# Attention on one core: score units merged to 18 steps a quad, score pairs in blocks of three

## The reference

```
x_proj = layernorm(x) @ Wqkv + bqkv                 # 16 heads of 16
att = where(causal, q @ k.T / sqrt(16), -inf)       # q, k, v = x_proj split and RESHAPED to (B, 16, T, 16)
y = softmax(att) @ v
x = x + y @ Wproj + bproj
```

## Time and profile before

| | us |
|---|---|
| median of 3 runs (lowest, highest) | 3928.14 (3921.84, 3932.45) |
| profiled execution, span | 3930.1 |
| attention, from the first pair to the last, about | 1077 to 3303 |

### The profile page before, as it was taken

One profiled execution on the slowest core, in us unless ns is written; L12 is line 12 of the kernel. 1 busy time (PEld: TensorE's weight loads), 2 busy tenths in 40 slices (PEclk: granted clock), 3 DMA queues, 4 the chain that ended last, 5 costly groups with the idle time before them and its releaser, 6 DMA issues. The chain is left out here.

```text
span 3930.1 us, 77952 instructions
## 1 busy us (share of the span) xinstructions
PE 3667.3 (93%) x26062; PEld 2353.8 (60%) x26062; DVE 2960.1 (75%) x9275; ACT 2237.0 (57%) x4407; POOL 1663.9 (42%) x2027
## 2 busy tenths in 40 slices
PE   6998999998689999999999999999999997999997
PEld 5887766665445555555555555555555554666664
DVE  8998577675677788788778878878877884576675
ACT  1100565555166666666666666666666665556654
POOL 2332132333445555554555545556455520132323
PEclk9999999999699999999999999999999998999999
DMA  2333122111877776877768777687876752121211
GB/s 71 102 101 103 43 65 65 46 57 35 158 112 114 112 117 107 121 109 115 123 108 116 117 112 118 105 126 104 117 122 110 101 71 61 34 69 60 65 39 49
DMA packets 701469, 361.31 MB, mean 92 GB/s; under 512 B 305072, under 2 KB 668080, under 8 KB 701104
## 3 DMA queue, kind: packets, MB, share of 16 engines
q1 hardware_dynamic: 701104, 356.65, 50.8%
HBM read 204.49 MB, written 150.99 MB: 90 GB/s over the span
## 5 line engine op out<-in xcount | busy, mean ns | idle before, releaser
L1839 ACT ACTIVATE att_probs<-att_s 128x512 f32<-128x512 f32 (+1 forms) x2560 | 1319.3, 557 | 755.3 <-PE att_s L1928 430.9
L1719 DVE CUSTOM_DVE_ANT_0 att_s<-att_s,att_above 128x384 f32<-128x384 f32 (+3 forms) x2048 | 958.0, 514 | 189.0 <-PE att_s L1958 188.9
L1980 PE MATMUL att_s<-att_qs,att_ks 49*128 49x512 f32 (+3 forms) x3072 | 917.9, 388 | 90.0 <-ACT att_probs L1839 29.1
L1958 PE MATMUL att_s<-att_ks,att_qs 48*128 48x512 f32 (+3 forms) x3072 | 964.2, 407 | 5.8 <-DVE att_maxima L1722 3.7
L1980 PEld LDWEIGHTS att_s<-att_qs,att_ks 49*128 49x128 f32 x3072 | 459.7, 185 | 650.9 <-ACT att_probs L1839 433.6
L1722 DVE TENSOR_REDUCE att_maxima<-att_s 128x1 f32<-128x512 f32 x1024 | 668.8, 682 | 225.6 <-PE att_s L1958 219.3
L2008 PE MATMUL att_o_ps<-att_probs,att_vs 128*32 128x512 f32 (+3 forms) x6144 | 632.1, 499 | 0.5 <-ACT att_probs L1839 0.5
L1958 PEld LDWEIGHTS att_s<-att_ks,att_qs 48*128 48x128 f32 x3072 | 487.6, 188 | 25.1 <-DVE att_maxima L1719 8.0
L1097 PE MATMUL ffn_h2p<-ffn_h,ffn_w 128*128 128x512 f32 x768 | 363.3, 595 | 3.0 <-ACT ffn_h L968 0.9
L1928 PE MATMUL att_s<-att_mask,att_places 64*128 64x64 bf16 (+1 forms) x3072 | 332.5, 205 | 0.0
L1719 DVE DVE_READ_ACCUMULATOR2_ANT att_maxima<- 128x1 f32 x2048 | 290.0, 142 | 0.0
(11 more groups left out here) (292 smaller groups left out, 6331.1 us busy)
## 6 DMA issues: line engine op xcount, KB each, us to landing
att_staged<-qk_scratch SPq DMA_DIRECT2D x768, 128.0 KB, 7.5
qk_scratch<-att_parts SPq DMA_DIRECT2D x128, 512.0 KB, 3.7
ffn_x<-x SPq DMA_DIRECT2D x64, 512.0 KB, 5.2
ssm_x<-in_L_attn_a_x_dram SPq DMA_DIRECT2D x32, 512.0 KB, 3.8
x<-ssm_y SPq DMA_DIRECT2D x32, 512.0 KB, 3.0
x<-ffn_y SPq DMA_DIRECT2D x32, 512.0 KB, 2.9
att_x<-x SPq DMA_DIRECT2D x32, 512.0 KB, 12.3
v_scratch<-att_v_tok SPq DMA_DIRECT2D x32, 512.0 KB, 3.4
```

Source lines behind the costliest of these rows:

```text
L1719: last = v.tensor_tensor_reduce(scores, scores, above[:, CH - w:CH], 1.0, -3.0e38, ALU.add, ALU.max, to)
L1839: a(probs[u % 2][2 * g + p][:, 0:n], bank[:, 0:n], ACT.Exp).then_inc(exp_done, 1)
L1958: last = mm(bank[:, col:col + w], rows_of(qs[buf], g, KROWS, p, BT * blk, BT * (blk + 1)), rows_of(ks[buf], g, KROWS, p, t0, t1), start=k ...
L1980: last = mm(bank[:, col:col + w], rows_of(ks[buf], g, SHIFT + 1, p, BT * j, BT * (j + 1)), rows_of(qs[buf], g, SHIFT + 1, p, t0, t1), star ...
```

## The change

- The two 256-wide units of `PASS2` become one of two pieces, so a quad has 9 units and 18 steps (36 halves), and each half of pass 2 has a partner of pass 1. The piece (6, 48, 64) belongs to the second half of the queries, so its product with V moves into `times_v` of unit 3 (`TIMES_V`).
- TensorE issues pairs in blocks of three. Only behind a block come an other work (in 8 of 12 blocks, `X_SLOTS`), then a `times_v` (9 a quad: `TIMES_V_SLOTS`, and the previous quad's last one behind block 0). Behind blocks 2, 3, 4, 8 and 10 come both.
- `probs` gets a third set, and an exponential waits for the `times_v` of three units back.
- VectorE and ScalarE order their tasks by halves instead of steps.

```diff
-    PASS2 = [[(0, 0, 32)], [(1, 8, 32), (3, 24, 32)], [(2, 16, 32)],
+    PASS2 = [[(0, 0, 32)], [(1, 8, 32), (3, 24, 32)], [(2, 16, 32), (6, 48, 64)],
              [(0, 32, 64)], [(1, 32, 64)], [(2, 32, 64)], [(3, 32, 64)], [(4, 32, 64)],
-             [(5, 40, 64), (7, 56, 64)], [(6, 48, 64)]]
-    FIRST_U2, LAST_U2 = (0, 3), (2, 9)
+             [(5, 40, 64), (7, 56, 64)]]
+    FIRST_U2, LAST_U2 = (0, 3), (2, 8)
+    TIMES_V = [[(u, n) for n in range(len(PASS2[u])) if (u, n) != (2, 1)] + ([(2, 1)] if u == 3 else [])
+               for u in range(len(PASS2))]
+    PROBS = 3
+    BLOCK = 3
+    X_SLOTS = (1, 2, 3, 4, 6, 8, 9, 10)
+    TIMES_V_SLOTS = {2: 0, 3: 1, 4: 2, 5: 3, 7: 4, 8: 5, 10: 6, 11: 7}
...
-        heads = [] if first and q == 0 else [(1, "heads", 0), (7 if q == 1 else 5, "heads", 1)]
-        finish = [] if first else {0: [(9, "turn", 0), (11, "out", 0), (13, "turn", 1), (15, "out", 1)],
-                                   1: [(3, "turn", 2), (5, "turn", 3), (9, "out", 2), (11, "out", 3)]}.get(q, [])
-        project = {0: [(3, 6), (7, 7)], 1: [(13, 0), (15, 1)], 2: [(3, 2), (7, 3), (9, 4), (11, 5), (13, 6), (15, 7)],
-                   3: [(3, 0), (7, 1), (9, 2), (11, 3), (13, 4), (15, 5)]}[q] if (more2 if q == 3 else more) else []
+        heads = [] if first and q == 0 else [(0, "heads", 0), (3 if q == 1 else 2, "heads", 1)]
+        finish = [] if first else {0: [(4, "turn", 0), (5, "out", 0), (6, "turn", 1), (7, "out", 1)],
+                                   1: [(1, "turn", 2), (2, "turn", 3), (4, "out", 2), (5, "out", 3)]}.get(q, [])
+        project = {0: [(1, 6), (3, 7)], 1: [(6, 0), (7, 1)], 2: [(1, 2), (3, 3), (4, 4), (5, 5), (6, 6), (7, 7)],
+                   3: [(1, 0), (3, 1), (4, 2), (5, 3), (6, 4), (7, 5)]}[q] if (more2 if q == 3 else more) else []
+        return [(BLOCK * X_SLOTS[n] / 2, kind, which)
+                for n, kind, which in sorted(heads + finish + [(n, "project", j) for n, j in project])]
...
-                            tasks += [(step, lambda unit=unit: maxima(4 * b + q + unit[0], unit[1]))]
+                            for g in (1, 0):
+                                tasks += [(step + (1 - g) / 2,
+                                           lambda unit=unit, g=g: maxima(4 * b + q + unit[0], unit[1], (g,)))]
...
-                    if g == 0 and (old or u >= 2):
-                        act.wait_ge(pv_done, UNITS2 * quad + u - 1)
+                    if g == 0 and (old or u >= PROBS):
+                        freed = u - PROBS + 1
+                        act.wait_ge(pv_done, UNITS2 * quad + (freed + 1 if u == 2 + PROBS else freed))
...
-                            tasks += [(step, lambda step=step, g=g: exponentiate(quad, q, step, g, not first or q > 0))]
+                            tasks += [(step + g / 2, lambda step=step, g=g: exponentiate(quad, q, step, g, not first or q > 0))]
...
-                    use = s2_use(q, step, g)
-                    if use >= 3 or not first:
-                        before = 3 if use >= 3 else (1, 4, 4)[use]
-                        pe.wait_ge(exp_done, 2 * STEPS * quad + 2 * step + g - before + 1)
+                    if s2_use(q, step, g) >= 3 or not first:
+                        pe.wait_ge(exp_done, 2 * STEPS * quad + 2 * step + g - 2)
...
+                            if (2 * step + g) % BLOCK != BLOCK - 1:
+                                continue
+                            part = (2 * step + g) // BLOCK
                             for n, (at, kind, which) in enumerate(events):
-                                if g == 0 and at == step - 1:
+                                if at == BLOCK * part / 2:
...
-                            if g == 0 and step % 2 and (step >= 3 or old):
-                                u = (step - 3) // 2
-                                if u >= 0:
-                                    times_v(quad, q, b, u, old)
-                                else:
-                                    times_v(quad - 1, (q - 1) % 4, b if q else b - 1, UNITS2 - 1, True)
+                            if part == 0 and old:
+                                times_v(quad - 1, (q - 1) % 4, b if q else b - 1, UNITS2 - 1, True)
+                            if part in TIMES_V_SLOTS:
+                                times_v(quad, q, b, TIMES_V_SLOTS[part], old)
```

More of the change, by code:

```diff
@@ L1236, in x_events @@
     def x_events(q, first, more, more2):
-        heads = [] if first and q == 0 else [(1, "heads", 0), (7 if q == 1 else 5, "heads", 1)]
-        finish = [] if first else {0: [(9, "turn", 0), (11, "out", 0), (13, "turn", 1), (15, "out", 1)],
-                                   1: [(3, "turn", 2), (5, "turn", 3), (9, "out", 2), (11, "out", 3)]}.get(q, [])
-        project = {0: [(3, 6), (7, 7)], 1: [(13, 0), (15, 1)], 2: [(3, 2), (7, 3), (9, 4), (11, 5), (13, 6), (15, 7)],
-                   3: [(3, 0), (7, 1), (9, 2), (11, 3), (13, 4), (15, 5)]}[q] if (more2 if q == 3 else more) else []
-        return sorted(heads + finish + [(s, "project", j) for s, j in project])
+        heads = [] if first and q == 0 else [(0, "heads", 0), (3 if q == 1 else 2, "heads", 1)]
[5 more added lines that the diff above has]
+                for n, kind, which in sorted(heads + finish + [(n, "project", j) for n, j in project])]
     def flags(b):
@@ L1283, in attention_phase @@
         full = [sb(f"full{k}", [P, CH]) for k in range(FULLS)]
-        probs = [[sb(f"probs{k}_{i}", [P, CH]) for i in range(4)] for k in range(2)]
+        probs = [[sb(f"probs{k}_{i}", [P, CH]) for i in range(4)] for k in range(PROBS)]
         o_sb = sb("o", [P, 2, CH])
@@ L1707, in low, with maxima @@
                         v.memset(carrier[:, :], 0.0).then_inc(freed, 1)
-                def maxima(quad, unit):
+                def maxima(quad, unit, groups=(1, 0)):
                     p, pieces, n = unit // len(PASS1), PASS1[unit % len(PASS1)], 2 * (UNITS1 * quad + unit)
-                    for g in (1, 0):
+                    for g in groups:
                         dve.wait_ge(s1_full, n + 2 - g)
@@ L1724, in maxima @@
                         last.then_inc(s1_free, 1)
-                    if unit % len(PASS1) == len(PASS1) - 1:
+                    if unit % len(PASS1) == len(PASS1) - 1 and groups[-1] == 0:
                         dve.wait_ge(s1_free, n + 2)
@@ L1834, in exponentiate @@
                     act.wait_ge(s2_full, 2 * STEPS * quad + 2 * step + g + 1)
-                    if g == 0 and (old or u >= 2):
-                        act.wait_ge(pv_done, UNITS2 * quad + u - 1)
+                    if g == 0 and (old or u >= PROBS):
+                        freed = u - PROBS + 1
+                        act.wait_ge(pv_done, UNITS2 * quad + (freed + 1 if u == 2 + PROBS else freed))
                     n = sum(HD * (t1 - t0) for _, t0, t1 in PASS2[u])
                     bank = s2_ps[s2_use(q, step, g) % 3]
-                    a(probs[u % 2][2 * g + p][:, 0:n], bank[:, 0:n], ACT.Exp).then_inc(exp_done, 1)
+                    a(probs[u % PROBS][2 * g + p][:, 0:n], bank[:, 0:n], ACT.Exp).then_inc(exp_done, 1)
                 def project(hb, j, index):
@@ L2001, in times_v @@
                         pe.wait_ge(v_loaded[s], 16 * (turn + 1))
-                    col = 0
-                    for n_piece, (j, t0, t1) in enumerate(PASS2[u]):
-                        w = HD * (t1 - t0)
+                    for n_piece, (of, n) in enumerate(TIMES_V[u]):
+                        j, t0, t1 = PASS2[of][n]
+                        col, w = sum(HD * (u1 - u0) for _, u0, u1 in PASS2[of][:n]), HD * (t1 - t0)
                         for i in range(4):
@@ L2008, in times_v @@
                             last = mm(o_ps[32 * i:32 * i + 32, HD * (t0 - first_t):HD * (t1 - first_t)],
[L2009 to L2012, removed]
+                                      vs[s][:, NBLK * head + j, :], probs[of % PROBS][i][:, col:col + w],
+                                      start=(u == FIRST_U2[half] and n_piece == 0),
+                                      stop=(u == LAST_U2[half] and n_piece == len(TIMES_V[u]) - 1))
                     last.then_inc(pv_done, 1)
```

## The result

| | before | after |
|---|---|---|
| median of 20 runs each, us | 3930.24 | 3947.15 |
| lowest, highest | 3921.84, 3947.27 | 3924.48, 3969.38 |
| time after / before, 95% interval | | 1.0039 [1.0025, 1.0052] |
| profiled execution, span | 3930.1 | 3961.0 |

What follows compares the result with a forecast made beforehand. TensorE sets the pace (busy 134.33 of 140.02 us in four quads), VectorE next. Work less 4.4 and stalls less 0.8 make 5.2 per four quads, x 16 = 83 us: 3930 - 83 - 2 = 3845 us, range 3795 to 3915.

Steps and rivals of the forecast that it cites:

- GpSimd in quad 3: Projection at half 20 waits for GpSimd's second transposed tile; chain stays, TensorE arrives up to 1 us earlier: 1.5, before 1.0.
- Saved work: TensorE's work without stalls falls by 0.8 + 0.3 = 1.1 us a quad, 4.4 in four quads.
- VectorE's statistics: About 1.8 us of VectorE work at step 6 of quads 0 and 2, costing 0.4 each in stalls.
- number 1: End of pass 2 in each quad: four single halves go with the merge of units, saving 0.8 us a quad.
- number 2: TensorE's pairs in blocks: 29 changes of kind instead of 36 per quad, saving 0.3 us, range 0 to 1.0.
- an other work followed by TV: Behind five blocks a quad: priced as a full leaving plus a full entering; bounds for the change 0 and 0.3.
- Evacuation and TV 3: Behind block 5, probabilities-times-V 3 waits for evacuation and exponential, about 0.2 us a quad, 0.8 in four.
- VectorE's releases: The waits view of four quads should show more VectorE releases than before (2.6).
- Row maxima: Half 2 waits for transferred row maxima, landing taken as 1.0: new stall of 1.1 in quad 2, 0.5 in quad 1.
- C: No change (3928): saved work turns wholly into VectorE waits, 1.3 us a quad; chance 0.06.
- B: Slower (about 4000): second row-maxima moves fall behind in SyncE's queue, half 2 stalls by 10 in four quads; chance 0.11.
- A: Half or more given back (3901): small new dependences at ends of quads 0 and 1, unpriced other-work-to-TV change; chance 0.20.

Runs made afterwards that it cites:

- e3: Changed kernel with GpSimd's layouts in q = 3 sorted behind the split of the second transposed tile that the projection needs; 3861.18 us, 0.9851 of the kernel before.
- e2: Changed kernel with SyncE's store of V for q = 2 moved behind the stack loads of q = 3; 3866.80 us, 0.9847 of the kernel before.
- e11: e1 with GpSimd's split first in q = 3, `LEAD` 5, VectorE's statistics later and q = 0's load of V behind the second row-maxima moves; 3842.98 us, 0.9770.
- e10: e3 with `LEAD` 5 instead of 4, VectorE's statistics at 7 instead of 6, and q = 0's load of V behind the second row-maxima moves; 3849.05 us, 0.9813.
- e1: Changed kernel without blocks: merge to 18 steps, third probabilities set and finer order stay, other works and TVs at old places; 3962.96 us, 1.0102.
- e9: e3 with SyncE's load of V in q = 0 moved to 15.5, behind the second moves of row maxima; 3859.71 us, 0.9829 of the kernel before.

## Why the prediction was wrong

**The step that failed** is the third of the stalls, GpSimd in quad 3: "It stays where it is, while TensorE now arrives up to 1 us earlier: 1.5 (before: 1.0)". Neither half holds. The chain does not stay: it hangs, through the layouts, the stack loads and SyncE's queue, on GpSimd's work of the quad before, and that quad became 2.2 us shorter (36.76 to 34.52) with its last split 0.2 later in it. The sum left the chain at its old distance from the quad's start; it moved by 4.0 us (10.33 to 14.30). And TensorE comes later, not earlier: half 20 starts 16.10 us into q = 3 (15.64 in e3), 15.13 before. At half 20 the cost was 4.3 us of pause and 2.2 of clock, 5.0 more than the 1.5 in the sum for a group of four quads. Thirteen groups have that wait, so it is about 62 us over the phase (57.1 of wait and 13 x 2.2 of clock, less 16 x 1.5), of the 102 between 3845 and 3947.15. With the chain cut (e2, e3), 1.9% or 74 us come back, 1.0039 against 0.9847 and 0.9851.

The clock had no term in the sum: half 20 to 21 was priced at full clock, and the loss by the low one was put at nothing without a reason. The Trainium skill, TensorE: Matmul & The Clock Gate, Part 1, says that the array runs at half rate unless its own activity opens the gate, and the trace agrees: 0.50 for 6.8 us behind the pause, and 1.00 when it had run again. In the four stretches of q = 1 that took 10.2 or 13.7 us.

**The other steps.**

- *Saved work, 1.1 us a quad*: e3 saves 6.0 in four quads by the medians (139.67 to 133.64) and 4.7 by the means (139.49 to 134.83). The forecast of 5.2 kept 1.5 for GpSimd, which e3 doesn't have, so like should be 6.7: the saving is there, but smaller, and e3's 3861.18 is 40 us above the 3821 that this makes. Two terms make about that. The third pair of q = 1 and the slow clock behind it cost 2.2 us in e3 (mean 33.59 against its shortest in these kernels, 31.4), where 0.5 was priced: 27 us. VectorE's statistics and the evacuation together cost 1.1 more than priced (below): 17 us. Of the parts of the saving, number 1 (the merge) carries it, and number 2 (fewer interruptions, 0.3) does not show: e11 without blocks is no slower than e10 with them. And the sum of work took the seventeen longer other works, priced 1.58 to 1.9, at 1.61 each, near their low end. The price of an other work followed by TV was right: block 3 of q = 0, with transposes and a TV, takes 0.34 + 0.41 + 2.04 = 2.79 us, where the like was priced 2.82.
- *Evacuation and TV 3*, 0.8 in four quads: the last pair of block 5 is left after 0.77 and 0.89 us in q = 1 and 3 against 0.43 in q = 0 and 2, which makes 0.8.
- *VectorE's statistics*, 0.4 in q = 0 and 2: the pairs at halves 15 and 16 leave 0.63 and 0.3 late, so 0.9.
- *VectorE's releases*, 2.6 in the four quads, are 2.0, and over the phase they fell, from 42.6 to 33.5 us.
- *Row maxima*: the landing, chosen as 1.0 without a row, came out near: half 2 starts 1.12 behind the end of the last issue wherever it waits for it; the stall in quad 2 was to be 1.1 and is 0.2, since VectorE's waits at halves 30 and 31 lengthen the way; in quad 1 it was to be 0.5 and is 1.5 in the median (half 1 to half 2 takes 1.87), and quad 3, which had none in the sum, has 0.4.

**The rivals.** The time lies nearest to C's 3928 and in direction with B, and it came through the queue that B names, with about the size from which B said that it decides (5.2 us in four quads); but B looked at the moves of row maxima in quads 0 and 2, and what was late was the stack loads behind a store that waits for GpSimd. A named small new dependences; more was given back than it had, and elsewhere. C's waits for VectorE do not show.

**Open.** Quads q = 1 last 31.4 to 39.0 us after. In the trace the four of 37.7 to 39.0 are the four with a stretch at 0.50, the other nine last 31.4 to 34.2; eleven of the thirteen start half 2 just 1.12 us behind the last issue of the moves, and no run cut that out by itself. The late load shortens q = 1, but e10 still has quads of 35 to 36. Why blocks of three bring nothing was not taken apart either. The waits view has a candidate, not tested: in e10, TVs wait 17.7 us for ScalarE (51 times), in e11 0.7 (once), about the 19 us (64 x 0.3) that the blocks were to save.

## What to carry to other kernels

When a stage becomes shorter, follow every chain that crosses its end (an engine's tail of work, the store that waits for it, the loads behind that store in one queue, who needs them), and measure its distance from the next stage's start anew; a task sorted by its place in the stage does not move with the end. Price a pause of some microseconds on TensorE (those of e1 were about 2 us) with its clock, not only with its length. Undo parts one at a time and together with the cure: the merge alone was 1.0% slower and, with four edits of order (e11), 2.3% faster.

## What the runs showed of the hardware

Behind each of the 13 waits for GpSimd of the changed kernel (57.1 us, so 4.4 us each) the clock was at 0.50 for 3.4 or 6.8 us, and there a projection took 2.90 instead of 1.65 us. Behind waits of up to 1.8 us in the same place (14 in 17.5 us) the kernel before has no such stretch; behind waits of up to 2.2 us for VectorE e1 has 22. Four stretches in q = 1 lasted 10.2 or 13.7 us, while TensorE worked on; no run shows what kept the clock down. Keeping TensorE busy with useless transposes in the wait gave 0.5% of the whole kernel back. The 512 KB load of V issues in 0.89 us itself, but the issue of the next large transfer behind it holds SyncE's queue: a load of 512 KB for 9.78 us (0.87 without it, e9), a store of 256 KB for 4.37 (0.44). What stands behind that in the queue, however small, cannot start before. What in the queue or the transfers makes it so, a full ring as the expectation of e9 has it or something else, is not shown.
